# One query tile quantised ahead instead of two, first scores of the cross-attention among the last products of the self-attention, norms without a negated mean

## What is computed

```python
x = x + _L1_attn_ref(_layernorm(x), W_dq, W_uq, ..., W_o)      # 16 heads of 16, causal
x = x + _L1_xattn_ref(_layernorm(x), ctx_2048, Wq, bq, Wkv, bkv, Wp, bp)
x = x + _L1_ffn_ref(_layernorm(x), w_cls, bias, w_gate_up, w_down)

def _L1_xattn_ref(x, cond, ...):
    q = (x @ Wq + bq); k, v = cond @ Wkv + bkv                 # 1024 queries, 1024 keys, 16 heads of 16
    q = fq_sym(q / 4, axis=-1)                                 # per token and head: round(x / s) * s, s = max|x| / 127
    k = fq_sym(k, axis=-1); v = fq_sym(v, axis=token)
    attn = fq_unsigned(softmax(q @ k.T), axis=-1)              # 0 to 255 steps of the row's maximum
    return (attn @ v) @ Wp + bp
```

## Time and profile before

| | |
|---|---|
| median of three runs | 540.27 us |
| profiled execution, its own time | 537.92 us |
| its span, first to last instruction | 536.2 us |
| busy in the span: PE, DVE, ACT, POOL | 434.5, 412.1, 341.9, 253.0 us |
| mean granted clock of TensorE | 0.966 of 2.4 GHz |

### The profile page before, as it was taken

The page is one execution under the profiler, slowest core; times in us unless marked ns, Lnnn a source line. Parts: engine busy times, 40 slices in busy tenths (PEclk is TensorE's granted clock), DMA queues, the critical chain, the costliest instruction groups (busy, mean ns, idle before and its releaser), DMA issues. The chain is left out here.

```text
span 536.2 us, 11095 instructions
## 1 busy us (share of the span) xinstructions
PE 434.5 (81%) x3915; PEld 285.1 (53%) x3915; DVE 412.1 (77%) x825; ACT 341.9 (64%) x636; POOL 253.0 (47%) x456
## 2 busy tenths in 40 slices
PE   7988857767988888587788888887888779899885
PEld 3536734445555565334445555454446338788664
DVE  5899898849599776999999999999995854542244
ACT  2664237944578465399999999999994114445340
POOL 5756210006089465304454464645322048888870
PEclk9999886989899998899999999999999999999999
DMA  8850000000006300399999999999995978996548
GB/s 284 240 185 12 0 2 1 1 0 1 1 1 109 51 1 1 41 173 182 154 183 178 188 177 185 184 193 194 182 189 112 307 238 227 238 238 122 86 75 246
DMA packets 169862, 69.46 MB, mean 130 GB/s; under 512 B 142352, under 2 KB 167632, under 8 KB 169808
## 3 DMA queue, kind: packets, MB, share of 16 engines
q1 hardware_dynamic: 162288, 58.53, 53.6%
q0 software_dynamic: 4704, 7.61, 7.8%
q10 hardware_dynamic: 2816, 2.62, 1.6%
HBM read 27.56 MB, written 7.62 MB: 66 GB/s over the span
## 5 line engine op out<-in xcount | busy, mean ns | idle before, releaser
L939 ACT ACTIVATE A<-ps,b,sq 128x1024 int16<-128x1024 f32 x128 | 153.2, 1203 | 15.5 <-POOL b L653 7.4
L1855 DVE TENSOR_REDUCE nm<-ps 128x1 f32<-128x1024 f32 x128 | 152.1, 1213 | 10.1 <-PE ps L1294 8.8
L1294 PE MATMUL ps<-big,ctx_sb 128*128 128x512 bf16 x256 | 78.4, 388 | 30.1 <-ACT A L939 26.3
L653 POOL TENSOR_SCALAR b<-nm,sq 128x1 f32<-128x1 f32 x120 | 31.8, 265 | 98.7 <-DVE nm L1855 68.5
L1365 PEld LDWEIGHTS ps<-VI,A 128*128 128x128 f16 x1024 | 42.9, 96 | 20.7 <-issue 3.4
L1930 DVE TENSOR_TENSOR AT<-AT,ps 128x128 f32<-128x128 f32 x32 | 9.2, 287 | 50.3 <-ACT AT L961 50.3
L719 POOL DMA_INDIRECT A<-x_rows,slot_token x32 | 35.3, 1103 | 25.3 <-DMA x_rows<-ctx_sb 15.9
L1365 PE MATMUL ps<-VI,A 128*128 128x16 f16 x1024 | 44.3, 170 | 0.6 <-DMA A<-A 0.3
L1294 PEld LDWEIGHTS ps<-big,ctx_sb 128*128 128x128 bf16 x256 | 15.2, 97 | 52.0 <-ACT A L939 41.3
L731 POOL DMA_INDIRECT sums<-XN,slot_token x22 | 35.4, 1610 | 7.6 <-issue 4.6
L990 PE MATMUL ps<-identb 128*128 128x512 bf16 x135 | 36.1, 413 | 2.6 <-POOL identb L518 2.6
(11 more groups left out here) (315 smaller groups left out, 1026.3 us busy)
## 6 DMA issues: line engine op xcount, KB each, us to landing
A<-in SPq DMA_DIRECT2D x32, 256.0 KB, 3.7
A<-in SPq DMA_DIRECT2D x32, 128.0 KB, 4.3
A<-in SPq DMA_DIRECT2D x2, 1024.0 KB, 14.0
A<-A SPq DMA_TRANSPOSE x112, 3.5
X<-in SPq DMA_DIRECT2D x2, 512.0 KB, 4.5
big<-in SPq DMA_DIRECT2D x1, 1024.0 KB, 9.2
ctx_sb<-in SPq DMA_DIRECT2D x1, 1024.0 KB, 16.4
sums<-zeros SPq DMA_DIRECT2D x2, 512.0 KB, 4.8
```

What stands on the lines that cost most here:

```text
L653: g.tensor_scalar(b5[:, n % 4:n % 4 + 1], nm5[:, n % 4:n % 4 + 1], sq5[:, q, h:h + 1], LN255, ALU.mult, ALU.add).then_inc(S["pbias5_ready" ...
L939: a.activation(Y5[:, n % YB, :], ps[:, 2 * ((n + 1) % 3):2 * ((n + 1) % 3) + 2, :], ACT.Exp, scale=sq5[:, q, h:h + 1], bias=b5[:, n % 4:n ...
L1294: done = T.matmul(ps[:, 2 * ((n + 1) % 3) + c, :], QT5[:, q % 2, h // 2, h % 2, :], KT5[:, h // 2, c * 512:(c + 1) * 512], start=True, sto ...
L1855: v.tensor_reduce(nm5[:, n % 4:n % 4 + 1], ps[:, 2 * ((n + 1) % 3):2 * ((n + 1) % 3) + 2, :].rearrange("p a c -> p (a c)"), AX.X, ALU.max, ...
```

## The change

It quantises one query tile ahead instead of two. Tile 0 keeps its path on DVE: the steps behind block 9 are cut to one tile, and its two pads move from behind block 13 to behind block 12. Tile 1 takes the path of the later tiles: its scales stand on DVE behind the maximum of unit 4, its product, rounding and copy on POOL at units 5 to 7, its transpose on SP behind that of unit 7's codes, its pads on POOL at units 11, 14, 17 and 22.

Scores of units 0 and 1 are written between PE's output products of blocks 13 and 14, their maxima on DVE between blocks 13 and 14. All biases are made on POOL. The subtraction on the query bias stands behind the biases of units 0 and 1, and the bias row of tile 1 is added at unit 2, not in the masks of the self-attention. The norm on POOL subtracts the mean itself, and `nmean` is gone. The diff, cut to its core:

```diff
-        PBIAS = list(range(LAG5, U5))
+        PBIAS = list(range(U5))
...
             query_T(0)
-            query_T(1)
             for n in range(U5):
                 sp.wait_ge(S["exp5_ready"], n + 1)
                 if n not in LAST5 and n not in BY_PE:
                     sp.dma_start_transpose(PT5[:, n % YB, :, :], Y5[:, n % YB, :]).then_inc(p5T_loaded[n % YB], 16)
                 q = at_unit(n, 13)
+                if n == 7:
+                    query_T(1)
...
                 g.tensor_scalar(veps[:, lo:hi], mv[:, lo:hi, 1], EPS, None, ALU.add).then_inc(S["rstd_e"], hi - lo)
-                done = 8 + NT + 2 * (first + hi - lo - 1)
-                if first < len(LN_ORDER):
-                    g.tensor_scalar(nmean[:, lo:hi], mv[:, lo:hi, 0], -1.0, 0.0, ALU.mult, ALU.add).then_inc(S["rstd_e"], hi - lo)
-                    pool.wait_ge(S["rstd_e"], done)
-                else:
-                    pool.wait_ge(S["rstd_e"], done - 1)
+                pool.wait_ge(S["rstd_e"], 8 + NT + first + hi - lo - 1)
...
-                g.tensor_scalar(XN[:, t, :], X[:, t, :], nmean[:, t:t + 1], rstd[:, t:t + 1], ALU.add, ALU.mult).then_inc(S["xn_ready"], 1)
+                g.tensor_scalar(XN[:, t, :], X[:, t, :], mv[:, t, 0:1], rstd[:, t:t + 1], ALU.subtract, ALU.mult).then_inc(S["xn_ready"], 1)
...
-            for n in range(LAG5, U5 + LAG5 + H):
+            for n in range(U5 + LAG5 + H):
                 q, at = (n - LAG5) // H, (n - LAG5) % H
                 ahead = q + 2 < NT
                 if n in PBIAS:
                     score_bias(n)
+                if n in (0, 1):
+                    pool.wait_ge(S["pbias5_ready"], n + 1)
+                    query_bias_part(n)
...
-                if at in PADS_H and 1 <= q < NT - 1:
+                if at in PADS_H and 0 <= q < NT - 1:
...
-                if at == Q5_H + 2 and ahead:
+                late = 3 * (q < 0)
+                if at == Q5_H + 2 + late and ahead:
                     scale_queries(q + 2)
...
-                if at == Q5_H + 5 and ahead:
+                if at == Q5_H + 5 - late and ahead:
                     add_bp(q + 2)
...
                     last.then_inc(S["o4_psum"], 1)
+                    if u == G4 - 3:
+                        scores5(0)
+                        scores5(1)
...
+                if u == 12:
+                    dve.wait_ge(S["pads_ready"], 10)
+                    dve.wait_ge(S["q5T_loaded"], 16)
+                    for e in range(2):
+                        v.tensor_copy(QT5[64 * e:64 * e + 64, 0, :, e, :], QR5[64 * e:64 * e + 64, 0, :, :]).then_inc(S["q5pad_ready"], 1)
                 if u == 13:
-                    dve.wait_ge(S["pads_ready"], 10)
-                    for t in range(2):
-                        dve.wait_ge(S["q5T_loaded"], 16 * 2)
-                        for e in range(2):
-                            v.tensor_copy(QT5[64 * e:64 * e + 64, t, :, e, :], QR5[64 * e:64 * e + 64, t, :, :]).then_inc(S["q5pad_ready"], 1)
+                    score_maximum(0)
+                    score_maximum(1)
...
-                    query_scales(0, 2, 0)
+                    query_scales(0, 1, 0)
...
-                    for t in range(2):
-                        v.tensor_scalar(kpart[:, t, :, 0:3, :], AT[:, t, :].rearrange("p (h d) -> p h d", d=HD).unsqueeze(2).to_broadcast([P, H, 3, HD]),
-                                        ROUND, -ROUND, ALU.add, ALU.add).then_inc(S["q5i_ready"], 1)
+                    v.tensor_scalar(kpart[:, 0, :, 0:3, :], heads.unsqueeze(2).to_broadcast([P, H, 3, HD]), ROUND, -ROUND, ALU.add, ALU.add).then_inc(S["q5i_ready"], 1)
+                    v.tensor_scalar(sq5[:, 0, :], sq5[:, 0, :], 0.25, None, ALU.mult).then_inc(S["q5_step"], 1)
...
-                    if n not in PBIAS:
-                        dve.wait_ge(S["max5_ready"], n + 1)
-                        if n >= 4:
-                            dve.wait_ge(S["exp5_ready"], n - 3)
-                        v.tensor_scalar(b5[:, n % 4:n % 4 + 1], nm5[:, n % 4:n % 4 + 1], sq5[:, q, h:h + 1], LN255, ALU.mult, ALU.add).then_inc(S["bias5_ready"], 1)
...
-                if at_unit(n, Q5_H + 1) is not None and q + 2 < NT:
-                    query_scales(q + 2, q + 3, 5 + 3 * q)
+                if n == 4 or at_unit(n, Q5_H + 1) is not None and q + 2 < NT:
+                    query_scales(q + 2, q + 3, 8 + 3 * q)
```

More of the change, by code:

```diff
@@ L354, in wait_side_read @@
                 eng.wait_ge(S[SIDE_READ[kind]], t + 1)
-        PBIAS = list(range(LAG5, U5))
+        PBIAS = list(range(U5))
         def padded(t, half, e):
-            return 4 * (t - 1) + 2 * half + e + 1
+            return 4 * (t - 1) + 2 * half + e + 3
         def wait_bias(eng, n):
@@ L461, in query_T @@
                 if t >= 2:
-                    sp.wait_ge(S["q5pad_ready"], 4 if t < 4 else padded(t - 2, 1, 1))
+                    sp.wait_ge(S["q5pad_ready"], 2 if t < 3 else padded(t - 2, 1, 1))
                 sp.dma_start_transpose(QR5[:, t % 2, :, :], kpart_rows[:, t, :]).then_inc(S["q5T_loaded"], 16)
@@ L636, in _, with query_bias_part @@
                     ln_rstd("q", 0, 2)
-                if n in (21, 23):
-                    add_bp((n - 21) // 2)
+                if n == 21:
+                    add_bp(0)
+            def query_bias_part(i):
+                lo = (64, 96)[i]
+                g.tensor_tensor(bqr[lo:P, :], bqr[lo:P, :], bq_hi[lo:P, :], ALU.subtract).then_inc(S["front_step"], 1)
+                pool.wait_ge(S["front_step"], 7 + i)
             pool.wait_ge(S["w_loaded"], 16 * 14)
             pool.wait_ge(S["uq5_ready"], 2)
-            pool.wait_ge(S["mask4_ready"], 2 * G4)
-            for i, lo in enumerate((64, 96)):
-                g.tensor_tensor(bqr[lo:P, :], bqr[lo:P, :], bq_hi[lo:P, :], ALU.subtract).then_inc(S["front_step"], 1)
-                pool.wait_ge(S["front_step"], 7 + i)
+            pool.wait_ge(S["q5_step"], 5)
             def score_bias(n):
@@ L658, in pad_queries @@
                 pool.wait_ge(S["q5T_loaded"], 16 * (t + 1))
-                pool.wait_ge(S["s5_psum"], H * (t - 1))
+                if t >= 2:
+                    pool.wait_ge(S["s5_psum"], H * (t - 1))
                 g.tensor_copy(QT5_words[64 * e:64 * e + 64, t % 2, pairs, e, :], QR5_words[64 * e:64 * e + 64, t % 2, pairs, :]).then_inc(S["q5pad_ready"], 1)
@@ L665, in scale_queries @@
             def scale_queries(t):
-                pool.wait_ge(S["q5_step"], 5 + 3 * (t - 1))
+                pool.wait_ge(S["q5_step"], 5 + 3 * t)
                 heads = AT[:, t, :].rearrange("p (h d) -> p h d", d=HD)
@@ L702, in _ @@
                     ln_apply("r", q - 1)
-                if at == Q5_H + 2 and ahead:
+                late = 3 * (q < 0)
+                if at == Q5_H + 2 + late and ahead:
                     scale_queries(q + 2)
-                if at == Q5_H + 3 and ahead:
+                if at == Q5_H + 3 + late and ahead:
                     round_queries(q + 2)
-                if at == Q5_H + 4 and ahead:
+                if at == Q5_H + 4 + late and ahead:
                     copy_queries(q + 2)
-                if at == Q5_H + 5 and ahead:
+                if at == Q5_H + 5 - late and ahead:
                     add_bp(q + 2)
@@ L934, in _ @@
                     wait_bias(act, n)
-                    if h == 0 and q >= 2:
-                        act.wait_ge(S["quant_step"], 5 * NT + 4 * (q - 2) + 4)
+                    if h == 0 and q >= 1:
+                        act.wait_ge(S["quant_step"], 5 * NT + 4 * (q - 1) + 4)
                     if n >= YB:
@@ L1209, in _, with scores5 @@
             pe.wait_ge(S["w_loaded"], 16 * 14)
+            def scores5(n):
+                h, q = n % H, n // H
+                if n == 0:
+                    pe.wait_ge(S["k5T_loaded"], 16 * NT)
+                    pe.wait_ge(S["q5pad_ready"], 2)
+                if n < 2:
+                    pe.wait_ge(S["exp4_ready"], 2 * G4 - 2 + n)
+                if q >= 1 and h % 8 < 2:
+                    pe.wait_ge(S["q5pad_ready"], padded(q, h // 8, h % 2))
+                if n == 2:
+                    pe.wait_ge(S["oq4_ready"], G4)
+                    pe.wait_ge(S["uq5_ready"], 2)
+                if n >= 3:
+                    pe.wait_ge(S["exp5_ready"], n - 2)
+                for c in range(2):
+                    done = T.matmul(ps[:, 2 * ((n + 1) % 3) + c, :], QT5[:, q % 2, h // 2, h % 2, :], KT5[:, h // 2, c * 512:(c + 1) * 512], start=True, stop=True)
+                done.then_inc(S["s5_psum"], 1)
             for i in range(G4 + 2):
@@ L1281, in _ @@
                 codes = n - 3 in BY_PE
-                if n < U5:
-                    h, q = n % H, n // H
-                    if q < 2 and h == 0:
-                        pe.wait_ge(S["q5pad_ready"], 4)
-                    if q >= 2 and h % 8 < 2:
-                        pe.wait_ge(S["q5pad_ready"], padded(q, h // 8, h % 2))
-                    if n == 2:
```

(14 more changed lines are left out.)

23 lines of the change are left out of this document (8 added, 15 removed).

## The result

The changed kernel takes 543.60 us (median of 16 runs, 541.17 to 547.02) where the kernel before takes 540.25 (16 runs beside them): ratio 1.007, 95% interval 1.0053 to 1.0087. It is slower by some 3.4 us; 536.0 was forecast.

A forecast was written before the change was run, and what follows sets the result against it. It took DVE as the fullest engine of cross-attention's loop of score products, maximum, bias and exponential. Terms 2.7 + 0.3 - 0.1 - 0.5 + 1.9 = 4.3 us brought the median from 540.27 to 536.0, range 534.4 to 538.9.

The forecast's parts named there:

- seam, up to maximum 2: Between self- and cross-attention: less DVE work brings the third maximum 2.7 us forward (bounds 1.9 and 3.3).
- units 2 to 8: Early cross-attention loop: biases leave DVE, tile 1's scales come back at unit 4; gain 0.3 us (bounds 0 and 0.7).
- The new subtract form I price as the add form: Layer norms on POOL: dropping the negated mean gains 0.27 us per norm, 1.9 in all, with the apply's price unchanged.
- the mean's slot: Negated mean on POOL, 0.27 us per norm: gained whole in six query norms and about one routing norm, 1.9 us.
- rival 2: Loop after unit 12: code transposes set a tile's pace, hiding the mean's slot; gain 2.4, time 537.9 us; chance 0.13.
- The stall at unit 11: POOL's pad waits for tile 1's late transpose, bias 12 behind it: 0.5 us lost (bounds zero and 2).
- rival 4: TensorE in cross-attention: the low clock does not come back, 9.1 us more per tile; one tile gives 545.1 us; chance 0.04.
- My test for it (eight units): Loop at low clock: 0.57 us lost per unit, so it decides from eight units on, from unit 8 to 16.
- scales, product and rounding: Seam on DVE, one tile instead of two: scales and product save 0.5 us, rounding 0.9.
- the two biases: Seam: biases of units 0 and 1 move from DVE to POOL, saving 2 x 0.25 = 0.5 us.
- The pads with their handover: Seam on DVE: padding one tile takes two copies instead of four, 1.0 us instead of 2.04.
- the wait for the query transpose: Seam on DVE: pads behind block 12 wait 0 to 0.7 us for the first query transpose; 0.2 taken.

The follow-up runs named there:

- e1: The changed kernel with the old norm (negated mean and add form) back on POOL: 539.72 us, ratio to before 0.9992.
- e12: e9 with the first two scores and maxima moved back behind block 15 of self-attention, as in e6: 536.17 us, ratio 0.9916.
- e6: e4 with scores and maxima 0 and 1 moved back behind block 15 of self-attention: 536.71 us, ratio 0.9964.
- e9: e4 with the mean negated on ACT, so POOL has neither the mean's slot nor the subtract form: 534.70 us, ratio 0.9895.
- e3: The changed kernel with query norms subtracting a mean in its own column, routing norms adding a negated mean in the mean's place: 545.44 us.
- e8: The changed kernel with the old norm and tile 1's transpose behind the code transpose of unit 5 instead of 7: 537.34 us, ratio 0.9961.
- e13: e7's kernel run and profiled again, the kernel before with all biases on POOL: 540.19 us, ratio 0.9998.
- e2: The kernel before with one part alone, no negated mean and the subtract form on POOL: 543.52 us, ratio 1.0075.
- e4: The changed kernel with the old norm, tile 1's queries quantised in the seam's idle time, transpose ahead of all code transposes: 537.26 us, ratio 0.996.
- e5: e4 with the negated mean made on POOL one bias later, right ahead of the apply: 536.53 us, ratio 0.9953.
- e7: The kernel before with one part alone, the biases of units 0 to 7 on POOL instead of DVE: 540.18 us, ratio 1.0027.

## Why the prediction was wrong

| term | forecast | changed kernel | where |
|---|---|---|---|
| seam, up to maximum 2 | -2.7 | -1.51 | table |
| units 2 to 8 | -0.3 | -0.33 | table |
| units 8 to 21 (pads, stall, one mean) | +0.33 | +2.97 | table |
| units 21 to the end (six means) | -1.62 | +1.97 | table |
| sum | -4.3 | +3.1 | |

**"The new subtract form I price as the add form"** is the step that turned the sign. Taking it as 0.55 us set a gain of 0.27 per norm; it is 1.24, so POOL pays 0.69 - 0.28 = 0.41 more in each norm, and a steady tile 0.29. The wait it opened is not the one the forecast looked at: the bias did come earlier, but the apply's length reached ACT through TensorE's transposes and the copy behind them, 0.60 in a tile. From unit 21 on, that is 3.6 of the 7.4 us between forecast and result; in units 8 to 21 another 0.73 (20.80 for e1's 20.07). The form stood in the trace of before on DVE only (line 1688: 404 ns, median of three), and DVE's price was no evidence for POOL. I should have given this operation both bounds, as I did for other unknown costs. The mechanism beside it was right: e12 differs from e6 by the mean's slot alone, moved to ACT, and its stage is 1.66 us shorter where seven slots were put at 1.9; e9 has the 22.56 us tile. So rival 2 (slot hidden) falls, apart from one pair of landings in e9 in which transposes did set the pace.

**The stall at unit 11, "I take 0.5"**, was short by 0.5, and what follows a stall was not in the sum. Exponential 12 went from 0.56 us ahead of before to 0.43 behind: 1.0 us. The transpose was issued at 238.28 and not at 235.4, since exponential 2 started at 228.14 where I had 225.8, and from then on the queue had no gap. Of these 2.9 us, 1.0 is the lateness of the whole stage and 1.2 what the seam fell short by, and both move bias 12 as well; some 0.7 is left, most of it in the queue, where one code transpose took 2.02 us to issue instead of 1.33. Then units 15 to 17 lost another 1.2 to 1.4 us at the low clock. The windows of the changed kernel:

```profile
240.00:245.00 5.00, 2.49 (x26) 1.02 (x24) 3.88 (x5) 3.58 (x5) 2.68 (x6) 1.00 1.02 191
245.00:249.00 4.00, 3.33 (x25) 2.43 (x27) 2.09 (x2) 3.12 (x8) 1.48 (x5) 0.58 1.02 191
```

TensorE was busy 2.49 us of the five ahead, and then stood near the 1.2 GHz level. This is rival 4 at a size that I did not give it: not a whole tile, but one stretch worth some 1.4 us. My test for it (eight units) was too coarse to see that, and the case that I held against it was one execution: in the second profile of the kernel before the low stretch lasted some 3 us longer. All three kernels with the late pad and no products to fill it had a stretch there (changed, e1, e3); of those without a late pad e8 and e13 had it too, and before, e2, e4, e5, e6, e7, e9 and e12 had none there. So the late pad may bring it on, but is not needed for it, and what exactly does stays open. The Trainium skill, "TensorE: Matmul & The Clock Gate", Part 1, calls it "run-variable" how many matmuls of one kernel run at the low clock until it is released; the two profiles of the kernel before agree (0.99 and 0.50 as far behind the bias adds). Why one execution of the bias-only kernel fell to the low clock in the middle of the loop and the other did not, no run shows.

**The seam, 2.7 forecast, 1.51 found.** From the bias adds to the block behind them it gained 1.36 (4.75 to 3.39), where scales, product and rounding were put at 1.4; the two biases gave 0.48 for 0.5. The pads with their handover gave 0.73 for 1.0 (2.08 to 1.35), the wait for the query transpose took 0.81 for 0.2, and self-attention's blocks 10 to 15 took 0.25 more (7.66 to 7.91), which was not forecast. The wait is the mis-sized term, and the landing its cause: 4.78 us, at the top of the range of the earlier trace rows. I took 0.2 of a wait that these landings put at 0 to 0.7. The range mixed two places: the first query transpose of the stage took 4.5 to 4.9 us in all fifteen profiles (4.59 in the one I had), while those of tiles 2 and 3 took 3.2 to 3.7 in thirteen of the fifteen. In all fifteen, a packet of the queue that loads instructions starts 2.5 to 2.8 us behind the issue of that first transpose, which is then still in flight (216.51 in the changed kernel). The page of the changed kernel counts 32 such packets of 16 KB:

```profile
q8 instruction: 32, 0.52, 0.4%
```

Of all transposes from 205 us on, 469 had such a packet start in their flight and landed 4.60 us behind their issue in the median, the other 1098 took 3.38. That is a coincidence in every trace, not yet a cause: no run moved such a packet. e4 shows that the wait can be filled at next to no cost (a seam of 15.62 for e1's 15.55).

**Right:** units 2 to 8, as closely as can be told (0.33 for 0.3, but the five profiles with this code took 7.73 to 8.12 us, a gain of 0.16 to 0.55); that the work of tile 1 on POOL is covered; that no gain hangs on the two early exponentials (e6). The expert stage's length, 131.94 for 131.42, is within the scatter of two profiles of one kernel.

## What to carry to other kernels

Removing an instruction by changing another's operation is two changes: price the new operation on that engine, from a row of that engine, or keep the old operation and let an idle engine make its operand. When work is put off to a later place in a queue, count its issue from when the work that fills the queue ahead of it really starts, and read a landing from a transfer in the same place of its queue; the seam had idle time on both engines in which it cost nothing. And compare stages between two cuts that both profiles share before believing a whole time that scatters by 4 us from lowest to highest.
